# Five lines through all layers instead of rounds: the written-out order of steps of a four-layer block on one core

## The reference, cut to what matters

```python
mod = silu(c) @ w_adaln + b_adaln            # six rows of 288 per batch: shift, scale, gate, twice
h = ln(x) * (1 + sc_msa) + sh_msa
q, k, v = split(h @ w_qkv + b_qkv)           # 16 heads of 18
attn = softmax(q @ k.T * 18 ** -0.5)
x = x + g_msa * ((attn @ v) @ w_proj + b_proj)
h = ln(x) * (1 + sc_mlp) + sh_mlp
x = x + g_mlp * mlp(h)                       # 288 -> 1152 -> gelu -> 288
```

## Time and profile before

| | |
|---|---|
| median of three runs | 1694.19 us |
| profiled execution, its own time | 1697.5 us |
| its span, first to last instruction | 1695.8 us |
| mean granted TensorE clock | 0.917 |
| TensorE matmuls / weight loads | 83% / 48% busy |
| VectorE, ScalarE, GpSimd | 62%, 47%, 20% busy |
| instructions | 31116 |

### The profile page before, as it was taken

How to read it: one execution, slowest core, us unless ns; L and a number is a source line. 1 busy time by engine, 2 the same in 40 slices (tenths; PEclk the granted TensorE clock), 3 DMA queues, 4 the chain that set the end, 5 groups by cost and what they waited for, 6 DMA issues and landing times. The chain is left out here.

```text
span 1695.8 us, 31116 instructions
## 1 busy us (share of the span) xinstructions
PE 1415.2 (83%) x12102; PEld 822.2 (48%) x12102; DVE 1051.0 (62%) x2500; ACT 804.6 (47%) x1519; POOL 346.3 (20%) x425
## 2 busy tenths in 40 slices
PE   3647897787899997999999999899886657897877
PEld 0324453443555553556566555565643424454445
DVE  4566654667687777766665464655656775667443
ACT  1443454365455656564625555545454442453542
POOL 0001031223323333223111222211220020121210
PEclk9768998888899998999999999999998878898988
DMA  4332233422111212123103123202020010100001
GB/s 129 87 129 69 63 97 104 152 97 70 59 41 72 80 55 71 48 87 108 17 27 99 52 87 108 57 33 68 8 67 18 19 60 6 33 7 19 19 21 43
DMA packets 79465, 105.35 MB, mean 62 GB/s; under 512 B 39237, under 2 KB 66390, under 8 KB 75990
## 3 DMA queue, kind: packets, MB, share of 16 engines
q1 hardware_dynamic: 77206, 100.99, 19.3%
q10 hardware_dynamic: 2112, 2.36, 0.4%
HBM read 86.57 MB, written 16.49 MB: 61 GB/s over the span
## 5 line engine op out<-in xcount | busy, mean ns | idle before, releaser
L1204 PE MATMUL P<-XT,W 128*128 128x512 f16 x1512 | 355.9, 387 | 0.4 <-ACT HQS L1949 0.4
L1350 PE MATMUL P<-W,H 128*128 128x288 f16 x864 | 255.9, 296 | 2.0 <-POOL H L2011 1.9
L1351 PE MATMUL P<-W,H 128*128 128x288 f16 x864 | 255.0, 295 | 0.0
L1352 PE MATMUL P<-W,H 128*128 128x288 f16 x864 | 254.8, 295 | 0.0
L2006 POOL TENSOR_TENSOR X<-X,TM 128x288 f32<-128x288 f32 x144 | 126.9, 884 | 602.2 <-DVE TM L1683 513.5
L1204 PEld LDWEIGHTS P<-XT,W 128*128 128x128 f16 x1512 | 142.9, 99 | 178.9 <-issue 27.6
L1941 ACT ACTIVATE G<-P 128x512 f32<-128x512 f32 x216 | 129.0, 597 | 120.5 <-PE P L1204 104.4
L1931 ACT ACTIVATE ARENA<-P 128x512 f32<-128x512 f32 x256 | 135.5, 602 | 86.9 <-PE P L1310 86.7
L1608 DVE TENSOR_REDUCE NM<-P 128x2 f16<-128x512 f32 x256 | 157.8, 685 | 15.1 <-PE P L1295 14.7
L2011 POOL TENSOR_TENSOR H<-G,H 128x512 f16<-128x512 f32 x100 | 120.2, 1205 | 194.4 <-ACT H L1942 189.5
L1204 PE MATMUL P<-WQ,XT 128*128 128x288 f16 x1008 | 145.7, 289 | 1.2 <-ACT XT L1863 0.5
(11 more groups left out here) (283 smaller groups left out, 2240.2 us busy)
## 6 DMA issues: line engine op xcount, KB each, us to landing
W<-scr_w SPq DMA_DIRECT2D x9, 1440.0 KB, 6.1
W<-scr_w SPq DMA_DIRECT2D x9, 1368.0 KB, 5.7
ADB<-scr_ada SPq DMA_DIRECT2D x24, 432.0 KB, 4.1
ADB<-scr_ada SPq DMA_DIRECT2D x24, 288.0 KB, 4.3
scr_w<-W SPq DMA_DIRECT2D x4, 1440.0 KB, 5.9
scr_w<-W SPq DMA_DIRECT2D x4, 1368.0 KB, 5.7
STG<-in_L_w SPq DMA_DIRECT2D x11, 432.0 KB
STG<-in_L_WT SPq DMA_DIRECT2D x11, 324.0 KB
```

Of the source, the lines that this page charges most:

```text
L1204: ins = e.matmul(o, l, r, start=k == 0, stop=k == len(pairs_) - 1)
L1350: e.matmul(o, hi, W2[:, 2 * m, :], start=False, stop=False)
L1351: e.matmul(o, hi, W2[:, 2 * m + 1, :], start=False, stop=False)
L1352: ins = e.matmul(o, lo, W2[:, 2 * m, :], start=False, stop=m == 8)
```

## The change

The functions `attention`, `across` and `fence` go. In their place stand five lines, each running through all three layers and all batches: `attends` (rank 0: scores, exponentials, products with V), `ends_` (0.5: normalisation, then `finish`), `tops` (0.8: maxima), `preps` (1: layer norm, Q, K, V), and `bg` (3). Two rotation lines of rank 5 are dealt beside them from the start and wait for their inputs. The stream is always in the deal, with rank 2 for an up half and -1 for a down half (9 before).

```diff
+        def deal(lines):
+            while True:
+                todo = [y for x in (*lines, *ms.line()) for y in x.tips()]
+                if not todo:
+                    return
+                now = [x for x in todo if x.when <= pe.clock + SLACK]
+                best = min(now, key=lambda x: x.rank) if now else min(todo, key=lambda x: x.when)
                 best.step()
...
-                    self.now = Line(self.piece(), 9)
+                    self.now = Line(self.piece(), 2 if self.half == 0 else -1)
...
+        every = [(L, b) for L in range(3) for b in range(B)]
+        preps = Line(chain(*(chain(*[wq_load(L)] * (L > 0), *(prep(L, b) for b in range(B))) for L in range(3))), 1)
+        tops = Line(chain(*(maxima_tokens(b) if L == 1 else maxima_rows(L, b) for L, b in every)), 0.8)
+        attends = Line(chain(*(attend_tokens(b) if L == 1 else attend(L, b) for L in range(3) for b in range(B))), 0)
+        ends_ = Line(chain(*(chain(*[wp_load(L)] * (L > 0), *(chain(settle_tokens(b) if L == 1 else settle(L, b), finish(L, b)) for b in range(B))) for L in range(3))), 0.5)
+        deal([attends, ends_, tops, preps, bg, *(Line(rotated(k), 5) for k in range(2))])
```

```diff
+            def tips(self):
+                if self.kids:
+                    self.kids = [x for x in self.kids if not x.over]
+                    if self.kids:
+                        return [y for x in self.kids for y in x.tips()]
+                return [] if self.over else [self]
```

A line that needs a bank no longer takes the one that comes free first at once. It waits, in the plan, until that bank is free:

```diff
+def slots(ring, n):
+
+    asked = -1.0
+    while True:
+        free = sorted((f for f in ring.free if f is not None), key=ends)
+        if len(free) < n:
+            yield "wait"
+        elif ends(free[n - 1]) <= asked or not free[n - 1]:
+            return
+        else:
+            asked = ends(free[n - 1])
+            yield list(free[n - 1])
```

Exponentials and gelu take turns. `attend` holds the turn for half a batch (`attend_tokens` for a whole one), `up` for an up half:

```diff
+        def hold(kind):
+            other = "gelu" if kind == "exp" else "exp"
+            turns["asks"].add(kind)
+            while turns["now"] or (turns["last"] == kind and (other in turns["asks"] or other == "gelu" and ms.half == 0 and ms.line())):
+                yield "wait"
+            turns["asks"].discard(kind)
+            turns["now"] = turns["last"] = kind
```

The tiles of the rotation move from the arena to the two staging buffers of the weights, and the fence goes:

```diff
-        Z = [last32[:, i * 256:(i + 1) * 256] for i in range(2)]
...
+        Z = [STG[i][0:D, 0:256] for i in range(2)]
+        MB = [STG[i][0:D, 256:256 + C] for i in range(2)]
+        OUT = [STG[i][:, 544:544 + 2 * C].rearrange("p (a c) -> p a c", c=C) for i in range(2)]
```

More of the change, by code:

```diff
@@ L96, in chain @@
         yield from p
+def slots(ring, n):
[9 more added lines that the diff above has]
+            yield list(free[n - 1])
 def slot(ring):
-    while ring.held():
-        yield "wait"
+    return slots(ring, 1)
 def two(ring):
-    while sum(f is not None for f in ring.free) < 2:
-        yield "wait"
+    return slots(ring, 2)
 def part(g, n):
@@ L408, in to_columns @@
         def to_columns(w, b, y, full, mixed=False):
+            while rXB[w].held():
+                yield "wait"
             i, _, free = rXB[w].take()
@@ new lines, in prep_tokens, with maxima_tokens, maxima @@
+            while qt_rd[u] is None:
+                yield "wait"
+            yield tuple(turned(g, *x) for g in range(2) for x in (("q", full_q, qb_rd, qt_rd[u]), ("k", full_k, kb_rd, kt_rd[u])))
+            tok["turned", 1, b] = made
+            qt_rd[u] = kt_rd[u] = v32_rd[u] = None
+            yield
+        def maxima_tokens(b):
+            while ("turned", 1, b) not in tok:
+                yield "wait"
+            u, made, mx = b % 2, tok["turned", 1, b], []
+            def maxima(first):
+                for c in range(first, 4, 2):
+                    yield from two(rP)
@@ L473, in prep_tokens @@
-                    rP.free[j] = [v]
-                    wr[name].append(v)
+                    for n, jj in enumerate((j, j2)):
+                        v = do(dve, "t_top", 0.69, c=c, n=n, j=jj, src=m, free=nm_rd[0])
+                        rP.free[jj] = [v]
+                        mx.append(v)
                     yield "free"
[L476 to L487, removed]
@@ new lines, in heads @@
+                while qt_rd[u] is None:
+                    yield "wait"
+                yield from slot(rP)
+                _, j, pf = rP.take()
+                m = do(pe, "qk_T", mm_cost(8, 128), name=name, n=n, j=j, src=[a, d], free=pf, ind=tok.get("ind"))
+                last[n] = [m]
+                yield [m]
+                v = copy("qt" if name == "q" else "kt", 1.03 + BIAS, 0.7, u=u, n=n, j=j, src=m, free=(qt_rd if name == "q" else kt_rd)[u])
+                rP.free[j] = [v]
+                made.append(v)
@@ L980, in householder, with rotated @@
             yield
-        def rotated(rZ, rM, rOut, first):
+        def rotated(first):
+            while "U" not in tok or "E" not in tok:
+                yield "wait"
             cur, e = tok["E"]
@@ L1113, in step @@
                     return
+                if isinstance(v, tuple):
+                    self.kids = [Line(g, self.rank) for g in v]
+                    for x in self.kids:
+                        x.when = self.when
+                    return
                 self.when = self.before if v == "free" else ends(v) if isinstance(v, list) else newest[0]
                 self.before = newest[0]
-        def deal(need, others=(), stream=False):
-            while not all(x.over for x in need):
-                lines = [x for x in (*need, *others, *(ms.line() if (stream() if callable(stream) else stream) else ())) if not x.over]
-                now = [x for x in lines if x.when <= pe.clock + SLACK]
-                best = min(now, key=lambda x: x.rank) if now else min(lines, key=lambda x: x.when)
-                best.step()
```

307 lines of the change are left out of this document (161 added, 146 removed).

## The result

The changed kernel takes 1654.8 us (median of four runs, 1652.87 to 1655.87) against 1694.55 us for the one before beside it. The ratio is 0.9762, interval 0.9746 to 0.9779. The forecast was 1534 us with a range of 1480 to 1650. The sign was right, the size was not, and the time lies above the range. One execution among the six of a_row37, further down, took 3417.05 us and is left out of its median.

The account below looks back on a forecast made before the run. TensorE, busy 83% of the span, was taken as the bound. Layer 2's first scores at 1173, plus 298 for layer 2 and 65 for the tail, made a 1536 us span, forecast as 1534 us, range 1480 to 1650.

Parts of the forecast that it names:

- a density of 0.93: From 145 us to layer 2's first scores: TensorE's full-clock work over time, 956.2 us of work taking 1028 us.
- layer 2's first scores: End of the part before layer 2: they start at 1173 us instead of 1252, 79 us gained.
- the tail: Finishing, last unit and last rotations after layer 2: 65 us instead of 85, a gain of 20.
- The reference stage 720 to 1190: Middle of the kernel before, lines dealt beside each other: its density of 0.95 was taken as what the planner reaches.
- The VectorE bound for a batch without MLP: Layer 2: such a batch is bound by VectorE's 27.67 us of work, taken as 30 us.
- Turns: Alternating exponentials and up halves: some 14 table loads fewer, taken as 0, bounds 18 us gained to 20 lost.
- Rival A: Turns hold the attention line back in layers 0 and 2: 1642 us; range 1590 to 1685, chance 0.19.
- rotations inside layer 2: Six of eight batches' rotations run during layer 2 through the staging buffers, shortening the end by 20 us.
- Rival C: Background line of Householder and exponential starves behind the stream, rotations come alone at the end: 1742 us; chance 0.05.
- Rival B: Denser than thought, 0.95 in both stages and layer 2 at VectorE's rate: 1493 us, under 1490; chance 0.10.
- Rival D: No change: engines wait for each other, density stays 0.81 in the whole first part, 1695 us; chance 0.04.
- The signs I named: Trace marks for a right forecast: strip, clock, first MLP product, layer 2 maxima spacing, rotation spread, table loads, busy times.

Follow-up runs that it names:

- a_row37: Changed kernel with a planned landing of 3.7 us instead of 2.2 for the DMA of the maxima's row: 1689.3 us, ratio 0.9950.
- a_nobranch: Changed kernel with the branches of a batch run one after another, lines and turns kept: 1763.11 us, ratio 1.0407.
- a_slack13: Changed kernel with SLACK -1.3 in place of -0.5: 1607.83 us, ratio 0.9485.
- a_bgfirst: Changed kernel with the background line (weights, Householder, exponential) at rank -2, ahead of all, instead of 3: 1651.09 us, ratio 0.9744.
- a_firstbank: Changed kernel with the old PSUM bank rule (queue at once on the bank free first), gate products also waiting for planned weights: 1743.23 us, ratio 1.0282.

## Why the prediction was right and wrong

**What failed: "I take a density of 0.93 for them", for the work between 145 us and layer 2's first scores.** It was 0.81 in 145 to 500 and 0.85 in 500 to 1200. At 0.93 the 287 us of work of the first stretch would take 308 instead of 355 us, and the 593 of the second 638 instead of 700. That is 47 and 62 us. After 1200 there were 368 us of work left, 80 more than the forecast had for layer 2 and tail (288 in 363 us). At 0.93 these 80 are 86 us, which gives 449, and it took 453. So this one term holds 109 of the 117 us by which the span was missed (1652.9 against 1536). The rest is small: the work came out at 1322 instead of 1308, the start had done 74 instead of 64.5.

The same 117 us by the three terms of the sum: layer 2's first scores at 1212.6 instead of 1173 (40 us), layer 2 from there to the end of its last products with V, near 1572, 359 us instead of 298 (61, and as long as before), and the tail 81 instead of 65 (16). Most of the miss shows in layer 2 because the forecast had everything else finished before it began. At a density of 0.84 between 145 and 1212 it was not: the attention has the highest rank and goes on to layer 2, and what stays behind lies in it: 10 columns, the exponential, and five down halves of the MLP (180 of the products L1444, 36 a unit) where the forecast had three units.

**Why 62 us in the middle.** The reference stage 720 to 1190 was not a fair sample. The prediction counted the Householder chain among what was dealt there, but the columns were over after the first 61 of its 470 us. The changed kernel has columns until 1332 us. With one column and SLACK -1.0 the middle reaches 0.92, with one of them 0.88 and 0.86. That the columns and the thin margin together hold the middle down is shown by these three runs. How the margin does it is known only as a smaller sum of waits. How a column does it is only read from the trace: a product in the list ahead of ready ones, a slowed clock behind it, a fuller VectorE (435 of 700 us against 325 of 620).

**Why 47 us in 145 to 500: open.** The variants have 0.73 to 0.83 there. The two best are a_nobranch, which is slower as a whole, and a_slack13. In this stretch the MLP weights come through two staging buffers, and modulation rows wait for landings. I did not try either.

**Layer 2 and tail: near in density, not in length, and not for the reason given.** After 1200 the density is 0.81, and the forecast's 288 us of work in 363 are 0.79. In layer 2 itself (1212 to 1572) it is 319.76 x 0.95 / 360 = 0.84 against 0.64 before; the forecast's 260 us in 298 are 0.87. I said separate lines would let the next batch's maxima run beside this one's scores. a_nobranch has those lines and the old waits. Without branches the stretch after 1200 has 443.46 x 0.88 / 562 = 0.69, as before. The gain needs the branches within a batch, a part that the prediction did not even list by itself. The bank rule, worth up to 88 us, it did not price either. Both had been shown in the diff. The VectorE bound for a batch without MLP (30 us) was not tested by itself; the smallest distance of two batches was 30.4 us.

**Turns: taken as 0 with 18 us gained as one end; 27 measured.** The working compared 63 loads with the turns. But five free lines without turns make 88 loads, and that is what the turns prevent: 52 loads x 1.28 us = 67 us of ScalarE, beside 27 us of the kernel's time. (With turns I had counted 24 loads at gelu; there are 18, since gelu follows gelu without a load between when no exponential is waiting.) ScalarE's busy time fell by 64 us (851 to 787), 1.23 us for each. The Trainium skill ("ScalarE: Activation LUTs", What ACT_TABLE_LOAD costs) has 2.66 us with the drain; an estimate by that figure would be 138 us. The trace has no room for a drain on either side of a load: the next activation starts 0.02 us behind it, and the one ahead of that same load ends 0.01 us before it:

```profile
803.08 1.09 ACT L1891 ACTIVATE ARENA<-P 128x512 f32<-128x512 f32 x2
```

Rival A, that the turns bind, is false, although the measured 1655 lies in the range that it was given (1590 to 1685) and near its 1642: without turns the kernel is slower, not faster. That its number came closer than the forecast's is luck.

**Tail: 81 us from 1572, 65 predicted; rotations inside layer 2: 20 predicted, 6 measured.** The rotations were ready too late, since the exponential ran from 1421 to 1552. Its products on EY:

```profile
L1453 PE MATMUL P<-EY x240: 217/219/362, 1454.9 to 1549.4; 64*64 64x64 f32 x120
```

**Rival C** named the place and missed the price in this kernel. A column took 12.8 us on average (817 us for 64), and L1459 passed the 1300 us that I had set as its mark. But the rotations still found room, and a_bgfirst gained 4 us, inside the uncertainty. Its price does show in a_firstbank. **Rival B** is out. **Rival D** described the early and middle density best (0.81 there, with new waits of TensorE on VectorE), but its sum assumed the same density for the middle and gave layer 2 the forecast's time; the measured time lies between D and the forecast.

**The signs I named.** First L1296 product of 512 columns 186.6 us, asked for before 185. Layer 2's transposes L1393 31 to 62 us apart, 45 in the mean (1207 to 1520), instead of 35 from 1165. Clock 0.935 instead of over 0.95. Table loads 36, under 50. Rotations over 80 us, not 250. The second and third point at the term that failed.

**The best version** is the change with SLACK -1.0: 1605.49 us, 5.3% under the kernel before and 49 us under the change as made.

## What to carry to other kernels

Take a density from a stage only for the same mix of work: ask what the reference stage did not contain, here a serial chain of small operations that the new stage carries throughout. Ask too what the new ranks leave undone when the next stage begins, since it is paid there. When an order is written out for engines that work in order, concurrency between large pieces is worth less than it looks (the lines alone lost 123 us). It pays once the small pieces of one batch are free to interleave (108 us) and no product is queued for a bank that is still held (88 us, most of them through work that was left for the end). Then look again at the margin by which inputs must be early, for what it is worth depends on the order: 1.0 us instead of 0.5 gained 49 us in the new one and lost 11 in the old.

## What was not expected of the hardware

A stand of 3.04 us for one small product costs more than its length. The granted clock is 1.00 in 970 to 976 us and 0.50, its lower level, in 980 to 986. Down products that started 0.12 to 0.13 us apart ahead of it start 0.24 us apart behind it, 18 of them, some 2 us more. Windows of the two stretches, then TensorE after that product, and ahead of it:

```profile
970.00:976.00 6.00, 6.00 (x34) 2.92 (x33) 3.68 (x8) 5.17 (x11) 0.00 (x0) 1.00 0.10 19
980.00:986.00 6.00, 5.85 (x21) 3.14 (x22) 2.60 (x13) 0.88 (x3) 0.77 (x1) 0.50 0.01 3
```

```profile
981.88 0.45 PE L1442 MATMUL P<-W,H 128*128 128x288 f16 x1
982.12 0.45 PE L1443 MATMUL P<-W,H 128*128 128x288 f16 x1
```
```profile
975.56 0.29 PE L1442 MATMUL P<-W,H 128*128 128x288 f16 x1
975.69 0.29 PE L1443 MATMUL P<-W,H 128*128 128x288 f16 x1
```

A load of ScalarE's table stays at 1.28 us whether 36 or 92 of them are in the kernel.
